# The local mask moved from a TensorE product to a ScalarE copy

## The reference

```python
q, k, v = x @ Wq, x @ Wk, x @ Wv                  # x normalised
o_lin = gla_scan(softmax(q), softmax(k), v, log_sigmoid(k) / 16)
scores = einsum('bhnqd,bhnkd->bhnqk', rope(q), rope(k)) / sqrt(128)
scores = where(mask, scores, -inf)                # own block of 64 and the one before, causal
y = softmax(scores) @ v
o = (0.5 * y + 0.5 * o_lin).astype(bfloat16) @ Wo
```

## Time and profile before

| | |
|---|---|
| median of 3 runs | 1945.89 us (1943.95 to 1946.04) |
| profiled execution | 1944.25 us, its span 1942.5 |
| TensorE busy | 1859.2 us, 96% |
| VectorE busy | 1486.0 us, 77% |
| ScalarE busy | 1236.8 us, 64% |
| GpSimd busy | 1264.9 us, 65% |
| chain that ended last | TensorE 62%, VectorE 18%, issue 14%, GpSimd 4% |

### The profile page before, as it was taken

How to read it: one execution, slowest core, us unless ns; L and a number is a source line. 1 busy time by engine, 2 the same in 40 slices (tenths; PEclk the granted TensorE clock), 3 DMA queues, 4 the chain that set the end, 5 groups by cost and what they waited for, 6 DMA issues and landing times.

```text
span 1942.5 us, 42961 instructions
## 1 busy us (share of the span) xinstructions
PE 1859.2 (96%) x11566; PEld 1235.4 (64%) x11566; DVE 1486.0 (77%) x3980; ACT 1236.8 (64%) x4840; POOL 1264.9 (65%) x1164
## 2 busy tenths in 40 slices
PE   4899999999999999999999999999999999999997
PEld 3667666766666666766766666766766654444443
DVE  5998888888888888888888888888899956302122
ACT  5677777777777777777777777777667645412121
POOL 2777777777777777777777777777767747212121
PEclk8999999999999999999999999999999999999999
DMA  6111111111111111111111111111201024000000
GB/s 220 55 36 43 41 45 43 43 44 44 43 43 43 42 42 42 43 47 42 42 42 42 42 42 42 42 42 42 84 30 30 23 71 147 33 0 22 0 22 22
DMA packets 85452, 90.52 MB, mean 47 GB/s; under 512 B 14216, under 2 KB 56456, under 8 KB 85384
## 3 DMA queue, kind: packets, MB, share of 16 engines
q1 hardware_dynamic: 85384, 89.71, 14.8%
HBM read 76.48 MB, written 13.18 MB: 46 GB/s over the span
## 4 chain that ended last, share of the span: by engine, by line
PE 62%; DVE 18%; issue 14%; POOL 4%; ACT 1%; DVEq 1%; DMA 0%; POOLq 0%; ACTq 0%
PE bank L1363 17%; PE bank L1352 8%; PE bank L1391 6%; PE bank L1334 4%; PE bank L1407 4%; PE bank L1428 4%; PE bank L1489 4%; PE bank L1400 3%; DVE f_s L1055 2%; PE bank L1318 2%; DVE f_nrm L1042 2%; PE bank L1417 2%; POOL hl L600 2%; PE bank L1507 2%; PE bank L1410 2%
## 5 line engine op out<-in xcount | busy, mean ns | idle before, releaser
L554 POOL TENSOR_TENSOR f_acc<-f_acc,f_s 128x512 f32<-128x512 f32 x429 | 547.5, 1276 | 32.6 <-POOL f_acc L554 0.4
L1363 PE MATMUL bank<-wh,xh 128*128 (+2 forms) x1024 | 334.9, 327 | 6.6 <-DVE cumh L1204 6.0
L1363 PE MATMUL bank<-wl,xh 128*128 (+2 forms) x1024 | 334.8, 327 | 0.0
L1363 PE MATMUL bank<-wh,xl 128*128 (+2 forms) x1024 | 334.6, 327 | 0.0
L538 POOL TENSOR_TENSOR pr<-pr,rp 128x512 f32<-128x512 f32 x128 | 133.2, 1041 | 241.8 <-DVE rp L977 241.5
L1055 DVE TENSOR_SCALAR f_s<-f_nrm 128x512 f32<-128x512 f32 x480 | 260.9, 603 | 3.5
L651 ACT ACTIVATE qe<-bank,nqm 128x128 f32<-128x128 f32 x512 | 180.9, 365 | 108.6 <-DVE qs L906 78.1
L1489 PE MATMUL bank<-xh,w 128*128 (+3 forms) x704 | 218.3, 379 | 1.4 <-ACT sg L832 1.4
L600 POOL TENSOR_TENSOR hl<-hf,hh 128x512 f16<-128x512 f32 (+1 forms) x44 | 51.3, 1167 | 231.9 <-ACT hh L838 231.9
L679 ACT ACTIVATE pr<-bank,pmx 128x128 f32<-128x128 f32 x512 | 180.8, 367 | 32.4 <-DVE pmx L970 24.3
L1214 DVE SCALAR_TENSOR_TENSOR hf<-bank,sg 128x512 f32<-128x512 f32 (+1 forms) x44 | 30.3, 689 | 220.5 <-PE bank L1489 205.9
(11 more groups left out here) (178 smaller groups left out, 4975.0 us busy)
## 6 DMA issues: line engine op xcount, KB each, us to landing
f_blk<-wa SPq DMA_DIRECT2D x33, 320.0 KB, 2.9
f_raw<-wb SPq DMA_DIRECT2D x33, 256.0 KB, 2.7
dequantised<-f_w SPq DMA_DIRECT2D x33, 256.0 KB, 2.0
w<-dequantised SPq DMA_DIRECT2D x33, 256.0 KB, 4.3
raw_qkv<-wq SPq DMA_DIRECT2D x29, 256.0 KB, 2.4
raw_o<-wo SPq DMA_DIRECT2D x29, 256.0 KB, 2.6
f_recb<-scales SPq DMA_DIRECT2D x99, 64.0 KB, 2.6
f_absb<-scales SPq DMA_DIRECT2D x99, 64.0 KB, 2.6
```

The source lines that it names most:

```text
L554: nc.gpsimd.tensor_tensor(f_acc[:], f_acc[:], f_s[:, step, :], ALU.add).then_inc(s["f_ad"], 1)
L1363: last = nc.tensor.matmul(dst, av, w[:, sl + c, lo:hi], start=(n == 0), stop=(n == 3 * NC - 1))
```

## The change

`mask_scores` is new on ScalarE, between `decays` and `copy_qrT`: a plain copy of the mask from `win` into the bank. TensorE no longer multiplies the mask by the identity, except for the very first tile; from the second on no matmul into `SC` carries the opening flag, and all four products add to what the bank holds.

```diff
+            def mask_scores(t):
+                if number(t) != 0:
+                    nc.scalar.activation(SC[:], win[:, 1, :] if t.p else win[:, t.i % 2, :], ACT.Copy)
...
                 if l1.real():
                     q_exps(l1)
                     decays(l1)
+                    mask_scores(l1)
                     copy_qrT(l1)
...
             q_exps(l1)
             decays(l1)
+            mask_scores(l1)
             copy_qrT(l1)
...
-                nc.tensor.matmul(SC[:], identb[:], win[:, 1, :] if t.p else win[:, t.i % 2, :], start=True, stop=False)
+                if number(t) == 0:
+                    nc.tensor.matmul(SC[:], identb[:], win[:, 0, :], start=True, stop=False, skip_group_check=True)
...
-                                                start=False, stop=(j == 3))
+                                                start=False, stop=(j == 3), skip_group_check=True)
```

## The result

The changed kernel takes 1912.82 us (median of 4 runs, 1912.52 to 1914.06), the kernel before beside it 1945.97 (median of 4, 1943.95 to 1946.93). The ratio is 0.9832, with a 95% interval of 0.9817 to 0.9848: faster by 1.7%, or 33 us. The prediction was 1913.6. The span went from 1942.5 to 1911.0.

What follows compares the result with a forecast made beforehand. VectorE and GpSimd blocking each other were taken as the bound: 0.94 + 0.30 = 1.24 us a step, 29.8 over 24 steps, plus 2.5 elsewhere, 32.3 together, giving 1913.6 us; range 1896 to 1938, the forecast's own 1906 to 1920.

Steps and rivals of the forecast that it cites:

- The bound: VectorE and GpSimd hold each other in a loop through kt that takes 47.6 us a step; TensorE's own sum is 46.0.
- f_safe's gap: Turn 0: f_safe asks 0.22 us earlier, passes before GpSimd's last addition with 0.09 to spare; VectorE 1.22 us earlier.
- What f_nrm gives back: Turn 0: f_nrm is blocked by qc until 953.11 instead of 954.05, so kt comes 0.94 us earlier, not 1.22.
- Turns 2 and 3: Turn 2's first f_s misses its gap by 0.15 us; turn 3's gets through one gap earlier, gaining 0.3 a step.
- two blocked f_s become three: Sign of being right: in turn 3 the number of f_s blocked by GpSimd's additions rises from two to three.
- ScalarE's copy: 127 mask copies on ScalarE, 0.53 us from start to start each (range 0.50 to 0.81), duration 0.60.
- The cover named for it: In turns 1 to 3 the copy fits in ScalarE's wait for L1318, on average 1.03 us; in turn 0 it is 0.22.
- All that lies outside the loop: The other 31 turns (start, late steps) have at most 6.8 us in them; 2.5 taken as gain.
- TensorE only: Rival, chance 0.09: every removed product comes off the time, 28 us, giving 1918, with f_safe still at 1.17.
- f_safe misses its gap: Rival: f_safe stays blocked in turn 0; 1936 with turn 3's gain (chance 0.12), 1943 without (0.10).
- More gaps are caught: Rival, chance 0.13: f_nrm passes before qc and TensorE is the bound all round, 13 us more gained, 1900.
- hardly any word from TensorE: The loop of kt, q's rotation, additions, f_s, rp and f_safe takes 47.6 us a step almost without TensorE.

Runs made afterwards that it cites:

- turn0_only: Changed kernel, but only the scores made in turn 0 get their mask by ScalarE, the others keep the product: 1922.34 us, period 46.61.
- turns123_only: Changed kernel, but the scores made in turn 0 keep their product, those of turns 1 to 3 get the copy: 1935.62 us, period 47.30.
- no_copy: Changed kernel without the ScalarE copy, so scores from the second tile on have no mask: 1910.83 us, period 46.25.
- both_masks: Kernel before, its mask product and opening flag kept, with the ScalarE copy added under it: 1947.19 us, ratio 1.0004.
- adds_earlier: Changed kernel with GpSimd's additions in turns 1, 2, 3, 0 set to 3, 2, 5, 4 instead of 1, 4, 5, 4: 1947.1 us.
- adds_earlier2: Changed kernel with GpSimd's additions in turns 1, 2, 3, 0 set to 3, 3, 4, 4: 1939.77 us, period 47.39.
- before_adds: Kernel before, mask by the product, with GpSimd's additions in turns 1, 2, 3, 0 set to 3, 2, 5, 4: 1957.42 us.
- nrm_late: Changed kernel with kt and merge ahead of f_dq in turn 1, and f_nrm with its two f_s moved behind that merge: 1925.3 us.
- add_behind_pr: Changed kernel with one addition (step 2) moved behind pr in turn 1, and f_col with f_safe ahead of gh in turn 0: 1910.11 us.
- late_safe: Changed kernel with an unread 128x128 memset on VectorE directly before f_col, to make f_safe ask later: 1934.89 us.

## Why the prediction was right

**The bound.** It named the pair of VectorE and GpSimd as what closes a step of 47.6 us, not TensorE with its 96%. turn0_only and turns123_only show that the sum of TensorE's work doesn't decide: the same 0.22 us of TensorE is worth 0.99 a step in turn 0, and 0.30 in all in the three other turns together. Why the three give no more is seen at the head of turn 0, in VectorE's qtT of before and of after:

```profile
941.78 0.68 DVE L955 TENSOR_TENSOR qtT<-bank,edT 128x512 f32<-128x512 f32 x1
...
875.56 0.67 DVE L961 TENSOR_TENSOR qtT<-bank,edT 128x512 f32<-128x512 f32 x1
```

It ends at 942.46 and 876.23, and TensorE's matmul that needs it starts at 942.51 and 876.29, in both kernels 0.05 to 0.06 later. So qtT decided that start before as well, though the timeline books no wait there, and TensorE's 0.66 could count only as far as qtT came earlier.

**f_safe's gap.** Predicted to be caught with 0.09 in hand; measured 0.09 (882.60 against 882.69), f_safe 0.17. From rp of turn 3 to f_safe's start the distance fell by 0.22 us, and from there to f_nrm's start from 4.19 to 3.19 (885.79 - 882.60): the 0.22 + 1.00 of the prediction. That this gap, and not something beside it, makes the time is shown twice: with the gap lost by 0.01 us the period goes back to 47.27, and with every product in place but f_safe moved earlier, the kernel before comes down from 47.60 to 46.76. The rule of the Trainium skill, "SBUF — State Buffer", Who interferes with whom, that whoever issues first holds the shared port pair for its whole instruction, agrees with the rows 849.38 and 896.65 above to 0.01 us.

**What f_nrm gives back.** Predicted 0.28: blocked by qc from 952.01 to 953.11. Measured 0.19 (the prediction gave too much back, by 0.09), f_nrm at 1.57 instead of 1.38. Against GpSimd's last addition qc starts 1.03 earlier (885.54 - 882.69 = 2.85, for 952.79 - 948.91 = 3.88), and not 0.94: with each of the two waits that fell away some 0.05 went beyond the wait that the row gives. GpSimd's qc starts just ahead of it, timeline of turn 0 of after:

```profile
885.54 1.27 POOL L520 TENSOR_TENSOR qc<-qc,qs 128x512 f32<-128x512 f32 x1
...
885.79 1.57 DVE L1048 TENSOR_TENSOR f_nrm<-f_raw,f_recb 128x512 f32<-128x512 f32 x1
```

So turn 0 gave 1.03, and 0.94 was expected.

**Turns 2 and 3.** In turn 2 the first f_s was to miss its gap by 0.15; it does, by 0.23. In turn 3 it was to catch one, for 0.30. VectorE's f_s there and GpSimd's addition of turn 2, against the earlier trace rows:

```profile
904.80 1.27 POOL L554 TENSOR_TENSOR f_acc<-f_acc,f_s 128x512 f32<-128x512 f32 x1
...
905.03 1.33 DVE L1061 TENSOR_SCALAR f_s<-f_nrm 128x512 f32<-128x512 f32 x1
916.31 0.51 DVE L1061 TENSOR_SCALAR f_s<-f_nrm 128x512 f32<-128x512 f32 x1
916.74 1.49 DVE L1061 TENSOR_SCALAR f_s<-f_nrm 128x512 f32<-128x512 f32 x1
918.16 1.49 DVE L1061 TENSOR_SCALAR f_s<-f_nrm 128x512 f32<-128x512 f32 x1
```

From kt's end in turn 1 to rp of turn 3 are 29.67 us, where they were 29.99: 0.32. Of the "two blocked f_s become three" only the number is wrong: one slips through at 0.51, two are blocked, one is free. turns123_only measures the same term alone, 0.30.

**ScalarE's copy.** 0.53 between starts predicted, 0.51 measured; its duration 0.64 for 0.60. Without it the kernel is at most 2 us faster (no_copy), and added to the kernel before it costs nothing that can be told (both_masks, 1.0004). The cover named for it, the wait for L1318's result, shrank by 46 us.

**The sum, and its one wrong term.** 24 steps gave 1110.3 us from f_safe of step 4 to that of step 28, where they took 1142.8: 32.5, predicted 29.8 (1.35 for 1.24 a step). All that lies outside the loop was to give 2.5 and cost 1.0: 0.2 before it and 0.8 behind it, where one f_safe misses its gap. I had put 2.5, out of at most 6.8, without reading where those turns stand. The two errors, +2.7 and -3.5, nearly cancel, in the profiled execution (1912.0 forecast, 1912.8 measured) and in the median (1913.6 and 1912.82). That nearness is luck and says nothing of how exact the working was; the sizes of the steps do.

**The rivals.** "TensorE only" would have come to 1918 by another way, with f_safe at 1.17; the row says 0.17, and turn0_only and turns123_only come out the other way round. "f_safe misses its gap" would have been 1936; the kernel where it misses by 0.01 us takes 1934.9. "More gaps are caught": f_nrm did not pass before qc.

**What was wrong in it.** The pair was to close its loop "with hardly any word from TensorE". But from L1327, which starts at 942.51, to the scores that release p_max at 946.86, 4.35 us of the step go through TensorE, and the gain of turn 0 begins on that stretch: only because p_max waits for the scores (0.55) could a product less make f_safe earlier. That kt belongs to the loop is not shown either: in the changed kernel kt 0.6 us earlier brought nothing, since the additions of turn 2 came later and the f_s took the 0.6 back. That edit moved f_dq as well, and no run has it on the kernel before. And the step from "this pair decides" to "so spread the additions" failed: four kernels with additions or f_nrm moved (adds_earlier, adds_earlier2, before_adds, nrm_late) were all slower than the one they were made from, by 10 to 34 us, and a fifth (add_behind_pr) gained too little to tell. The pair's cost is the conflicts along the whole step, and in these kernels an instruction moved out of one put it, or another, into the next. Which order has the fewest stays open.

## What to carry to other kernels

When VectorE and GpSimd both work on SBUF, read VectorE's durations for outliers before its idle time: a ten-element instruction that takes 1.17 us is a wait that the chain of waits books as work, and the start and end of GpSimd's instructions beside it say how much earlier it must ask to get through. An edit on a third engine that looks worth 0.22 us a turn was worth 1.0 in one turn and 0.3 in the three others together, according to whether it carries such an instruction over an edge; work that out in each turn apart, and expect an edge of 0.1 us to be fragile: 0.09 us more on VectorE lost it in 22 of 24 steps. Don't conclude from such a loop that spreading the work will help: each instruction that is moved has to be set against its new neighbours too.

## What the runs showed of the hardware

- The edge is sharp: f_safe asking 0.01 us after the addition's start costs 1.28 us, 0.01 before it 0.17 (late_safe).
- Between two additions of GpSimd the gap was 0.09 us wide (882.60 to 882.69), and one f_safe or one f_s got in. An f_s behind it is blocked: in turn 3 an f_s of 0.51 us is followed by two of 1.49. Not every instruction is: the reciprocal behind f_safe, which reads one operand, ran beside the addition that had started at 882.69. The addition that an f_s overtook is itself recorded a little longer, 1.33 for 1.27; the one that f_safe overtook took 1.27 in the changed kernel (882.69) and 1.31 in late_safe (896.66).

```profile
882.81 0.22 DVE L1037 RECIPROCAL f_col<-f_safe 128x10 f32<-128x10 f32 x1
...
918.03 1.33 POOL L554 TENSOR_TENSOR f_acc<-f_acc,f_s 128x512 f32<-128x512 f32 x1
```

- ScalarE's copy from bf16 in SBUF into the bank took 0.64 us, the one of the same size from the bank to SBUF 0.60 when it was alone and 0.64 right behind another. All 127 lie within 7 ns (least, median, most):

```profile
L669 ACT ACTIVATE bank<-win x127: 631/635/638, 47.0 to 1538.2; 128x512 f32<-128x512 bf16 x103, 128x512 f32 x24
```

- Products without the opening flag (L1398) add to what ScalarE's 127 copies wrote into the bank, from the second tile on, after one tile whose product opened the bank.
